# The linear attention's output projection in three passes of rounded halves

## The reference, cut to what matters

```
x = x + cross_attention(layernorm(x), ctx_1024, ...)
x = x + linear_attention(layernorm(x))          # this case
x = x + mixture_of_experts(layernorm(x))        # top 2 of 8 experts

def linear_attention(x):                        # 16 x 64 tokens of 512, 16 heads of 32
    q = elu(x @ Wq.T) + 1;  k = elu(x @ Wk.T) + 1;  v = x @ Wv.T
    kv = einsum('bnhd,bnhm->bhdm', k, v);  k_sum = k.sum(axis=1)
    out = einsum('bnhd,bhdm->bnhm', q, kv) / (einsum('bnhd,bhd->bnh', q, k_sum) + 1e-6)
    return out.reshape(b, n, d) @ Wo.T          # the output projection
```

## Time and profile before

| | |
|---|---|
| median of 3 runs | 2445.7 us (2445.54 to 2445.78) |
| the profiled execution's own time | 2445.41 us |
| its span, first to last instruction | 2443.7 us |
| mean granted TensorE clock | 0.985 of full |
| TensorE busy, share of the span | 96% |
| the 8 output projections (L2014) | 1923.6 to 1999 us |
| maps of the linear attention (L1843) | 1847.6 to 1891.9 us |
| first matmul of the experts | 2028.33 us |

### The profile page before, as it was taken

The page is one execution under the profiler, slowest core; times in us unless marked ns, Lnnn a source line. Parts: engine busy times, 40 slices in busy tenths (PEclk is TensorE's granted clock), DMA queues, the critical chain, the costliest instruction groups (busy, mean ns, idle before and its releaser), DMA issues. The chain is left out here.

```text
span 2443.7 us, 41270 instructions
## 1 busy us (share of the span) xinstructions
PE 2353.4 (96%) x14585; PEld 2081.6 (85%) x14585; DVE 1259.5 (52%) x2126; ACT 1094.5 (45%) x1867; POOL 1126.3 (46%) x474
## 2 busy tenths in 40 slices
PE   8999999999999999999999999999988977999997
PEld 6799889889898989888898989889867757999986
DVE  3255555555555555555555555555575455455542
ACT  3345444445454545444454444444453214444442
POOL 2255555555554555555555555555561024232333
PEclk9999999999999999999999999999999988999999
DMA  4311111212111111212211121212301027455543
GB/s 157 97 53 49 42 49 46 62 42 63 47 53 48 42 50 46 63 40 64 57 42 49 43 61 33 77 33 67 99 29 37 37 85 196 146 162 150 159 144 78
DMA packets 146897, 177.07 MB, mean 72 GB/s; under 512 B 82160, under 2 KB 105584, under 8 KB 146672
## 3 DMA queue, kind: packets, MB, share of 16 engines
q1 hardware_dynamic: 136960, 147.11, 20.3%
q10 hardware_dynamic: 4608, 16.78, 2.2%
q0 software_dynamic: 5104, 10.24, 2.2%
HBM read 134.85 MB, written 39.22 MB: 71 GB/s over the span
## 5 line engine op out<-in xcount | busy, mean ns | idle before, releaser
L469 POOL TENSOR_TENSOR k_parts<-k_t,k_parts 64x1602 fp32r<-64x1602 f32 x128 | 426.1, 3329 | 445.7 <-DVE k_parts L561 445.6
L937 PE MATMUL ps_kv<-ctx_hi,wk_hi 128*128 128x256 f32 (+1 forms) x1536 | 461.2, 300 | 7.4 <-DVE ctx_lo L758 7.4
L937 PE MATMUL ps_kv<-ctx_hi,wk_lo 128*128 128x256 f32 (+1 forms) x1536 | 440.6, 287 | 0.0
L937 PE MATMUL ps_kv<-ctx_lo,wk_hi 128*128 128x256 f32 (+1 forms) x1536 | 439.1, 286 | 0.0
L625 DVE TENSOR_TENSOR probs_t<-ps_pt,probs_t 128x512 fp32r<-128x512 f32 x376 | 207.9, 553 | 440.9 <-ACT probs_t L807 438.6
L483 POOL TENSOR_TENSOR v_parts<-v,v_parts 128x832 fp32r<-128x832 f32 x120 | 267.3, 2228 | 321.9 <-ACT v_parts L825 320.7
L937 PE MATMUL ps_kv<-wv_hi,ctx_hi 128*128 128x512 f32 (+1 forms) x832 | 343.2, 413 | 1.9 <-DVE wv_lo L728 1.9
L937 PE MATMUL ps_kv<-wv_hi,ctx_lo 128*128 128x512 f32 (+1 forms) x832 | 327.5, 394 | 0.0
L937 PE MATMUL ps_kv<-wv_lo,ctx_hi 128*128 128x512 f32 (+1 forms) x832 | 327.4, 393 | 0.0
L795 ACT ACTIVATE k_t<-ps_kv,bk_sb 128x256 f32<-128x256 f32 (+1 forms) x384 | 186.0, 484 | 309.5 <-PE ps_kv L937 304.8
L937 PEld LDWEIGHTS ps_kv<-ctx_hi,wk_hi 128*128 128x128 f32 x1536 | 291.6, 190 | 10.3 <-issue 8.6
(11 more groups left out here) (283 smaller groups left out, 4011.3 us busy)
## 6 DMA issues: line engine op xcount, KB each, us to landing
ctx_raw<-ctx_dram SPq DMA_DIRECT2D x81, 512.0 KB, 3.8
w_raw<-w_dram SPq DMA_DIRECT2D x64, 512.0 KB, 3.8
rows_in<-zeros SPq DMA_DIRECT2D x150, 128.0 KB, 3.3
w_raw<-w_dram ACTq DMA_DIRECT2D x32, 512.0 KB, 4.0
ctx_raw<-ctx_dram SPq DMA_DIRECT2D x16, 644.0 KB, 4.3
q_blocks<-q_parts SPq DMA_DIRECT2D x256, 32.0 KB, 1.9
rows<-rows_in SPq DMA_DIRECT2D x8, 768.0 KB, 4.9
q_parts<-probs_t SPq DMA_DIRECT2D x16, 256.0 KB, 2.0
```

What stands on the lines that cost most here:

```text
L469: nc.gpsimd.tensor_tensor(k_parts[64 - 64 * s:128 - 64 * s, :], k_t[par][64 * s:64 * s + 64, g, :], k_parts[64 * s:64 * s + 64, :].bitcast ...
L937: last = nc.tensor.matmul(o, still, moving, start=(k == 0 and i == 0), stop=(k == DT - 1 and i == 2))
```

## The change

The output projection becomes a `product()` of halves. The transposed heads are split from PSUM: ScalarE writes `att_hi`, then VectorE subtracts it from the bank into `att_lo`. The weight is split as the others are: ScalarE rounds it in the map loop at n == 11, once the 10 maps up to the last of the queries are made (its halves lie where the query weight's halves were), and GpSimd subtracts as a third `split_weight` before its constants. The raw weight is loaded to 80 KB in the shared memory, where the cross attention's output weight was, so that its load waits for the projection of the last token tile. TensorE's three waits on `att_copied` become waits on `att_lo_done`.

```diff
+        self.lwo_hi, self.lwo_lo = at("lwo_hi", weight, F32R, 48 * KB), at("lwo_lo", weight, F32R, 56 * KB)
+        self.lwo_raw = at("lwo_raw", weight, F32, 80 * KB)
...
-        room("att_room", ... + [(f"att_t{i}", [P, DT, P], F32) for i in range(2)],
+        room("att_room", ... + [(f"att_{part}{i}", [P, DT, P], F32R) for part in ("hi", "lo") for i in range(2)],
-        self.lwo_sb = sb("lwo_sb", weight)
...
+        QUERIES_MADE = MAPS.index(("q", DT - 1, 1)) + 1
...
 # SP
-            sp.dma_start(m.lwo_sb[:], lwo.rearrange("(t p) n -> p t n", p=P)).then_inc(late_loaded, 16)
             sp.dma_start(m.router_sb[:], router.rearrange("p (t e) -> p t e", t=DT)).then_inc(late_loaded, 16)
+            sp.wait_ge(last_tile, PROJECTED)
+            sp.dma_start(shared.lwo_raw[:], lwo.rearrange("(t p) n -> p t n", p=P)).then_inc(late_loaded, 16)
...
 # GpSimd
+            split_weight(shared.lwo_lo, shared.lwo_raw[:], shared.lwo_hi, 2)
-            pool.wait_ge(w_lo_done, 2)
+            pool.wait_ge(w_lo_done, 3)
...
 # ScalarE, map loop
+                if n == QUERIES_MADE + 1:
+                    act.wait_ge(late_loaded, 32)
+                    act.wait_ge(made, QUERIES_MADE)
+                    nc.scalar.copy(shared.lwo_hi[:], shared.lwo_raw[:]).then_inc(w_hi_done, 1)
...
 # ScalarE, steps
-                    nc.scalar.copy(att_t[r % 2][:], ps_r).then_inc(att_copied, 1)
+                    nc.scalar.copy(att_hi[r % 2][:], ps_r).then_inc(att_hi_done, 1)
...
 # VectorE, steps, behind the heads and ahead of assign and of x2's update
+                r = t - ATT_T
+                if 0 <= r < TT:
+                    dve.wait_ge(att_hi_done, r + 1)
+                    nc.vector.tensor_tensor(att_lo[r % 2][:], ps_r, att_hi[r % 2][:].bitcast(F32), ALU.subtract
+                                            ).then_inc(att_lo_done, 1)
...
 # TensorE
-            pe.wait_ge(w_lo_done, 2)
+            pe.wait_ge(w_lo_done, 3)
             pe.wait_ge(late_loaded, 32)
...
                     if r >= 1:
-                        pe.wait_ge(att_copied, r)
+                        pe.wait_ge(att_lo_done, r)
...
                 if 0 <= r < TT:
-                    pe.wait_ge(att_copied, r + 1)
+                    pe.wait_ge(att_lo_done, r + 1)
...
-                    for g in range(DT):
-                        last = nc.tensor.matmul(ps_proj[:], att_t[r % 2][:, g, :], m.lwo_sb[:, g, :],
-                                                start=(g == 0), stop=(g == DT - 1))
-                    last.then_inc(proj_done, 1)
+                    product(ps_proj[:], (att_hi[r % 2], att_lo[r % 2]), (shared.lwo_hi, shared.lwo_lo)).then_inc(proj_done, 1)
...
-                    pe.wait_ge(att_copied, min(TT, r + 1 + TURN - ATT_T))
+                    pe.wait_ge(att_lo_done, min(TT, r + 1 + TURN - ATT_T))
```

More of the change, by code:

```diff
@@ L1128, in __init__ @@
              [(f"{n}{i}", [P, BLOCK], F32) for n in ("silu", "y") for i in range(2)])
-        room("att_room", [(f"att{i}", [P, D], F32) for i in range(2)] + [(f"att_t{i}", [P, DT, P], F32) for i in range(2)],
+        room("att_room", [(f"att{i}", [P, D], F32) for i in range(2)] + [(f"att_{part}{i}", [P, DT, P], F32R)
+                                                                 for part in ("hi", "lo") for i in range(2)],
              [("down", [P, RB, D], F32)])
         self.at = placed
-        self.lwo_sb = sb("lwo_sb", weight)
         self.router_sb = sb("router_sb", [P, DT, E])
@@ L1176, in attend_route_and_experts @@
         lwv_raw = xs[:, DT:2 * DT, :]
-        low, expo, kv_blocks, att, att_t = ([m.at[f"{n}{i}"] for i in range(2)]
-                                            for n in ("low", "expo", "kv_blocks", "att", "att_t"))
+        low, expo, kv_blocks, att, att_hi, att_lo = ([m.at[f"{n}{i}"] for i in range(2)]
+                                            for n in ("low", "expo", "kv_blocks", "att", "att_hi", "att_lo"))
         v_two = [xs[:, 2 * i:2 * i + 2, :].rearrange("p t d -> p (t d)").rearrange("p (g b c) -> p g b c", g=DT, b=2)
@@ L1275, in attend_route_and_experts @@
             sem("kv_done"), sem("blocks_done"), sem("heads_done"), sem("att_done"))
-        att_turned, att_copied = sem("att_turned"), sem("att_copied")
+        att_turned, att_hi_done, att_lo_done = sem("att_turned"), sem("att_hi"), sem("att_lo")
         proj_done, x_added = sem("proj_done"), sem("x_added")
@@ L1417, in slot, with split_weight @@
                     add_rows(s - 1, 1 - par, RB)
-            def split_weight(name, raw, k):
+            def split_weight(lo, raw, hi, k):
                 pool.wait_ge(w_hi_done, k + 1)
@@ L1423, in split_weight @@
                     pool.wait_ge(w_lo_done, k)
-                nc.gpsimd.tensor_tensor(w_lo[name][:], raw, w_hi[name][:].bitcast(F32), ALU.subtract).then_inc(w_lo_done, 1)
-            split_weight("lwk", shared.lw_raw[:], 0)
-            split_weight("lwv", lwv_raw, 1)
-            pool.wait_ge(w_lo_done, 2)
+                nc.gpsimd.tensor_tensor(lo[:], raw, hi[:].bitcast(F32), ALU.subtract).then_inc(w_lo_done, 1)
+            split_weight(shared.lwk_lo, shared.lw_raw[:], shared.lwk_hi, 0)
+            split_weight(shared.lwv_lo, lwv_raw, shared.lwv_hi, 1)
+            split_weight(shared.lwo_lo, shared.lwo_raw[:], shared.lwo_hi, 2)
+            pool.wait_ge(w_lo_done, 3)
             nc.gpsimd.memset(all_ones[:], 1.0).then_inc(pool_consts, 1)
```

## The result

The changed kernel took 2442.06 us (median of 18 runs, 2437.31 to 2444.39) against 2445.97 us before (18 runs, 2444.59 to 2450.38). The ratio is 0.9981, 95% interval 0.9974 to 0.9988: by the ratio 4.6 us less (2.9 to 6.4), by the medians 3.9 us less. The interval leaves out 1, so the kernel is faster, by about 0.2%. The time lies inside the stated range (2436.5 to 2443.4), short of the 6.1 us of the sum, and above the 2438.1 to 2440.8 that the prediction called its forecast.

A forecast was written before the change was run, and what follows sets the result against it. TensorE, busy 96%, was taken to bound the kernel, with all eight projections on the path. 4.1 us (six projections) plus 2.05 (two late ones), nothing elsewhere, gave 6.1 us off: median 2439.6 us, range 2436.5 to 2443.4.

The forecast's parts named there:

- rivals 1 and 2: Late projections wholly at 1.2 GHz, 2442.4 us, chance 0.13; one more experts' group at the low clock, 2441.9 us, chance 0.11.
- the forecast proper: Whole kernel: 4.9 to 7.6 us off, 2438.1 to 2440.8 us, chance 0.55.
- the prediction's own border: Whole kernel: 2440.8 us, some 0.2% or 4.9 us off, as the border of faster; faster had chance 0.70.
- All eight projections are on the path: Steps 4 to 8: TensorE is full; from step 9: VectorE waits for the projection, so all eight count.
- 0.69 us for each at full clock, 4.1 us for six: First six projections: 3.44 us of float32 product becomes 2.75 us each; bounds 3.5 to 4.7 us in all.
- The two late projections shrink in proportion, 2.05 us: Steps 10 and 11, partly at 1.2 GHz: 4.98 and 5.25 us shrink by 1.0 and 1.05 us.
- The third reading in the prediction: Two late projections: the slow part lasts as long as before, the rest shrinks; 0.69 us each, 1.4 in all.
- The subtraction costs nothing, 0.74 us to spare in step 9: VectorE's eight added subtractions, 0.69 us each, hidden by the projection; without that cover they cost 5.5 us.
- The weight's load, rounding and split cost nothing: Map loop: ScalarE's rounding ends 0.2 us before the next exponential, GpSimd's halves come 5 us early; 0 to 0.3 us.
- What follows the steps: Tables, first rows and experts hang on the last choice of experts and move earlier as a whole; first load 6 us earlier.
- The third and fourth: Rivals: late projections keep full clock, 2436.9 us, chance 0.12; rounded passes cost 0.215 us like float32, 2438.0 us, chance 0.03.

The follow-up runs named there:

- the float32 variant: The changed kernel with its projection made of float32 matmuls again, splits, waits and moved load kept: 2446.73 us against 2446.06 before, ratio 1.0003.

## Why the prediction was right, and where its sum failed

- *The range and the forecast.* The measured 2442.06 us lies in the range because the range takes in rivals 1 and 2; it is 1.3 us above the upper end of the forecast proper (2440.8), and by the prediction's own border, to which it gave 0.70, it falls with those that were given 0.24. (The range's upper end, 2443.4, is 1.0 us above rival 1 and not the half microsecond that the text says; the measured time is below either.)
- *All eight projections are on the path.* Right: from x4 to x9 the change takes 3.4 us off five distances, 0.68 each. TensorE doesn't wait up to x8; between x8 and x9 it waits 0.77 us for the choice of experts, in both kernels.
- *0.69 us for each at full clock, 4.1 us for six.* Right: 2.76 us in the chain, and 4.07 us up to x9 in the first profile. The 4.9 us of the second have 0.8 us by luck, from the last token tile's product.
- *The two late projections shrink in proportion, 2.05 us.* This is the step that failed. They gave 0.71 us in the chain of the first profiles (4.98 + 5.25 against 4.46 + 5.06), and 0.4 to 0.7 us by the updates' distances. The third reading in the prediction, that the slow part keeps its length (1.4 us), was nearest, and still too high: the slow part grew, from 6.3 to 7.6 us by the estimate above. With the gaps filled the same two projections gain 0.68 us each, so what failed is what was assumed of the clock, not what was assumed of the products.
- *The subtraction costs nothing, 0.74 us to spare in step 9.* Right: 0.94 us measured; taking it away gains nothing, four more of it cost 8.8 us.
- *The weight's load, rounding and split cost nothing.* Right: 0.29 us spare on ScalarE (0.2 forecast), and the float32 variant with all of them is at 1.0003.
- *What follows moves as a whole.* Nearly: the time behind the rows is 418.8 and 419.1 us against 419.7 and 419.3, a gain of about half a microsecond that was not forecast and is no larger than its spread. The first rows themselves come 4.4 and 5.3 us earlier after the start of the block than in the first profile of before, not 6.
- *Rivals.* The first, both late projections at 1.2 GHz throughout, gives 2442.4, close to the measured 2442.06, but it is not what happened: each kept a fast part, and the two took 9.52 us, not 11. The third and fourth didn't happen. The second is not seen in the two profiles of the changed kernel, whose second group took 5.67 and 5.25 us against 6.46.

In the profiles, the mean of two before and two after, the change's own places give 0.7 us up to x4, 3.4 us to x9 and 0.6 us to x11, 4.6 us before rounding. The whole block is 5.4 us shorter (601.7 and 601.3 to 596.4 and 595.8); the rest is 0.4 us of the last token tile and 0.5 us of the experts, less 0.1 us up to the rows. The timed ratio, 4.6 us with an interval of 2.9 to 6.4, agrees with both. The mean granted clock over the 18 runs after the change is 0.984, that of the kernel before 0.985 on each of three chips: the lower clock is in the timed runs too, and not only in the profiles.

## What to carry to other kernels

Where a float32 product of 128 x 512 x 512 is on the path, three rounded passes take a fifth off it, provided the two extra splits find gaps; read those gaps from the row behind which they will stand, one for each engine. Price a matmul that is preceded by idle time apart from the others: what it gains depends on the clock level it will have, and a proportional share of its slow duration was too much here. If a stretch alternates between TensorE and another engine, see first whether the clock falls there; filling all the gaps, around the first expert too, was worth as much as the change itself (5.2 us on the kernel before), while on the changed kernel the fillings of the steps alone showed in the profiles and not clearly in the times.

## What the runs showed of the hardware

The granted clock fell to 1.2 GHz during or right behind gaps of 2.3 us (two pieces) and 2.9 us, and stayed there for most of the next projection; in step 10 of the first profile the last three matmuls were fast again. With float32 products the clock still stood at 2.4 GHz after the 2.9 us (0.24 us for the matmul behind them, in three profiles); with three passes it had fallen by then (0.34 or 0.35 us behind the same 2.9 us, in three profiles). Matmuls whose result nobody reads, put into those gaps, held it at 2.4 GHz, with gaps of 0.2 to 0.4 us left. Together with the fillings around the first expert they took the changed kernel from 0.9981 to 0.9962 on one chip.

A product of 128 x 512 x 512 took 3.44 us from float32 operands and 2.75 us as three passes of rounded halves, both at granted clock 1.00. VectorE's subtraction with one input in PSUM took 0.69 us in all eight steps.

An unchanged stretch of 1842 us ended up to 3.8 us apart in 14 profiles of this family of kernels. For effects of 0.2% a single profile's span is no measure. The distance from x4 to x9 repeats to 0.02 us in two profiles of one kernel; those from x9 to x10 and to x11 differ by up to 1.1 us each, and their sum by 0.2 us.
